# Graph attention and a normalised adjacency product: attention's transfers cut into tile-paced pieces, and the last z part of two sums put off

## What is computed

```python
# layer 0: attention with 16 heads of 32 columns
seq = (x @ W_seq).reshape(N, 16, 32)
score1, score2 = einsum(seq, a1), einsum(seq, a2)          # [head, row]
scores = leaky_relu(score1[:, :, None] + score2[:, None, :], 0.2)
scores = scores + (1.0 - adj)[None] * -65500.0
hidden = einsum('hij,jhd->ihd', softmax(scores, -1), seq).reshape(N, 512)
x = layernorm(x + elu(hidden @ W_out + b_out))
# layer 1: adj as coefficient and, symmetrised and normalised, as matrix
A = (adj + adj.T) * 0.5 + eye
A = dinv[:, None] * A * dinv[None, :]
x = layernorm(x + (adj @ A) @ x)
```

## Time and profile before

| | before |
|---|---|
| median of 3 runs | 788.06 us (787.59 to 788.43) |
| the profiled execution | 786.61 us |
| its span in the trace | 784.8 us |
| PE busy | 749.7 us (96%) |
| VectorE busy | 554.7 us (71%) |
| ScalarE busy | 409.9 us (52%) |
| GpSimd busy | 130.1 us (17%) |

### The profile page before, as it was taken

The page is one execution under the profiler, slowest core; times in us unless marked ns, Lnnn a source line. Parts: engine busy times, 40 slices in busy tenths (PEclk is TensorE's granted clock), DMA queues, the critical chain, the costliest instruction groups (busy, mean ns, idle before and its releaser), DMA issues.

```text
span 784.8 us, 29353 instructions
## 1 busy us (share of the span) xinstructions
PE 749.7 (96%) x13731; PEld 552.4 (70%) x13731; DVE 554.7 (71%) x799; ACT 409.9 (52%) x302; POOL 130.1 (17%) x142
## 2 busy tenths in 40 slices
PE   6999799988999999999999999999999999999997
PEld 2444699988999999999999999444434444444443
DVE  2887899998988999999999983687772211333233
ACT  2874887986977888788897880333321111000000
POOL 0000113012320211101111001364433100000000
PEclk9999799999999999999999999999999999999999
DMA  7992510255313111011110121599119800001111
GB/s 304 413 406 103 235 57 5 84 110 110 56 60 84 58 58 36 26 58 58 58 58 4 58 71 31 97 186 175 54 31 172 119 0 1 18 36 41 41 40 41
DMA packets 17770, 71.65 MB, mean 91 GB/s; under 512 B 2016, under 2 KB 2016, under 8 KB 13408
## 3 DMA queue, kind: packets, MB, share of 16 engines
q1 hardware_dynamic: 13040, 52.99, 17.7%
q0 software_dynamic: 4608, 16.78, 14.1%
HBM read 77.89 MB, written 8.65 MB: 110 GB/s over the span
## 4 chain that ended last, share of the span: by engine, by line
PE 78%; DVE 15%; issue 5%; ACT 1%; DMA 1%; POOL 0%; DVEq 0%; POOLq 0%; SPq 0%; ACTq 0%
PE bank L631 13%; PE bank L534 12%; PE bank L533 12%; PE bank L531 11%; PE bank L618 11%; PE bank L467 7%; PE bank L579 7%; DVE RZ L852 5%; PE bank L587 3%; DVE RG L871 2%; DVE RG L867 2%; DVE RP L816 1%; PE bank L571 1%; DVE MT L892 1%; DMA RZ<-in_L_gnn_W_seq_dram 1%
## 5 line engine op out<-in xcount | busy, mean ns | idle before, releaser
L531 PE MATMUL bank<-RP,RG 128*128 128x66 f16 x4096 | 388.8, 193 | 6.9 <-DVE RG L871 3.6
L534 PE MATMUL bank<-RP,MT 128*128 128x66 f16 x4096 | 388.7, 194 | 3.6 <-issue 3.6
L531 PEld LDWEIGHTS bank<-RP,RG 128*128 128x128 fp8e4 x4096 | 386.3, 98 | 8.3 <-DVE RG L871 3.6
L533 PE MATMUL bank<-RP,RG 128*128 128x66 f16 x4096 | 388.7, 195 | 2.1 <-issue 2.1
L534 PEld LDWEIGHTS bank<-RP,MT 128*128 128x128 fp8e4 x4096 | 386.4, 98 | 3.2 <-issue 3.2
L533 PEld LDWEIGHTS bank<-RP,RG 128*128 128x128 fp8e4 x4096 | 386.4, 97 | 2.7 <-issue 2.7
L689 ACT ACTIVATE RZ<-RZ,TAB 128x2048 int8<-128x2048 f32 x160 | 306.6, 1988 | 15.3 <-DVE RG L867 14.5
L852 DVE TENSOR_SCALAR RZ<-RZ,TAB 128x2048 int8<-128x2048 f32 x96 | 132.3, 1378 | 0.0
L867 DVE TENSOR_TENSOR RG<-RZ,MT 128x512 int32<-128x512 int32 x160 | 121.7, 760 | 0.1
L631 PE MATMUL bank<-RZ,MT 128*128 128x512 f16 x512 | 110.7, 379 | 2.2 <-DVE MT L1023 2.2
L391 POOL TENSOR_TENSOR RP<-SEQ,TAB 128x528 f32<-128x528 f32 x32 | 52.2, 1652 | 331.8 <-DVE RP L818 256.7
(11 more groups left out here) (103 smaller groups left out, 593.2 us busy)
## 6 DMA issues: line engine op xcount, KB each, us to landing
RG<-in_adj_t_dram SPq DMA_DIRECT2D x16, 1024.0 KB, 10.6
RZ<-s_rows_dram SPq DMA_DIRECT2D x16, 1024.0 KB, 5.8
seq_copy_dram<-SEQ SPq DMA_DIRECT2D x1, 4224.0 KB, 14.2
S2Q<-in_adj_p_dram POOLq DMA_DIRECT2D x8, 512.0 KB, 6.3
S2Q<-in_adj_tp_dram POOLq DMA_DIRECT2D x8, 512.0 KB, 11.3
RZ<-in_x_dram SPq DMA_DIRECT2D x16, 256.0 KB, 3.5
RP<-in_adj_p_dram POOLq DMA_DIRECT2D x8, 512.0 KB, 7.1
RP<-in_adj_tp_dram POOLq DMA_DIRECT2D x8, 512.0 KB, 13.8
```

The costliest lines, as they stand in the source:

```text
L531: mm(pb[bank][:, c:c + 2 * DV], step, high, start=(j == 0 and i % IB == 0), stop=(j == NT - 1), skip_group_check=True)
L533: mm(pb[bank][:, c:c + 2 * DV], step, low, start=False, stop=(j == NT - 1), skip_group_check=True)
L534: last = mm(pb[bank][:, c + DV:c + 3 * DV], mask, edge, start=False, stop=(j == NT - 1), skip_group_check=True)
```

## The change

The first four panels, the s1 rows, the copy of the sequence values and the output weights travel in pieces of a quarter (the copy: an eighth), and each piece but those of the first two rows waits for a value of `g_ready`, the count of masked tiles. Panel e is loaded in head 4 + 2e, accumulated in head 5 + 2e, and gets its diagonal after that; before, panel after panel followed in every head from `prep(3)` on. VectorE's wait for the copy moves from ahead of head 1 to the first `hidden_head`. In the last stage `take_back(t)` stands ahead of `low_z(t)`, the last of the 16 z parts of the first two output sums is added after both have their first 15, and panels 10 to 15 are loaded, accumulated and completed in a staggered order. `NE` = 4 replaces `NQ` in two places without a change of value.

```diff
+            def load_s1(h, q):
+                i = slice(q * (N // NS), (q + 1) * (N // NS))
+                sp.dma_start(S1B[:, h % 2, i], s1_rows[h:h + 1, i].broadcast_to([P, N // NS])).then_inc(s1b_in[h % 2], 16)
...
             sp.wait_ge(tabs_done, 1)
-            sp.dma_start(seq_copy[:, :], SEQ[:, :, :, :].rearrange("p t h d -> p (t h d)")).then_inc(seq_stored, 16)
-            with sp.Fori(1, H // 2) as p:
-                for u in range(2):
-                    h = p * 2 + u
-                    sp.wait_ge(z_ready, h * NV - NV)
-                    sp.wait_ge(g_ready, h * NT - NT)
-                    load_s1(h, u)
+            for q in range(NC):
+                sp.wait_ge(g_ready, q * (NT // NC))
+                ts = slice(q * (NT // NC), (q + 1) * (NT // NC))
+                sp.dma_start(seq_copy.rearrange("p (t h d) -> p t h d", t=NT, h=H)[:, ts, :, :], SEQ[:, ts, :, :]).then_inc(seq_stored, 16)
+            for h in range(2, H):
+                sp.wait_ge(z_ready, (h - 1) * NV)
+                for q in range(NS):
+                    sp.wait_ge(g_ready, (h - 1) * NT + 3 * q)
+                    load_s1(h, q)
...
-            sp.dma_start(WO, w_out.rearrange("(k p) d -> p k d", p=P)).then_inc(wout_in, 16)
+            for k in range(KC):
+                sp.wait_ge(g_ready, (H - 1) * NT + 3 * k)
+                sp.dma_start(WO[:, k, :], w_out[k * P:(k + 1) * P, :]).then_inc(wout_in, 16)
...
+            def load_pieces(t, h):
+                for q in range(NS):
+                    blocks = slice(q * (NT // NS), (q + 1) * (NT // NS))
+                    gp.wait_ge(g_ready, h * NT + 3 * q + 1)
+                    gp.dma_start(panel(t)[:, blocks, :], adj_p[t][:, blocks, :]).then_inc(panel_in[t], 16)
+
+            def add_pieces(t, h):
+                gp.wait_ge(panel_in[t], 16 * NS)
+                for q in range(NS):
+                    blocks = slice(q * (NT // NS), (q + 1) * (NT // NS))
+                    gp.wait_ge(g_ready, h * NT + 3 * q + 1)
+                    gp.dma_start(panel(t)[:, blocks, :], adj_tp[t][:, blocks, :], accum_op=ALU.add).then_inc(panel_sum[t], 16)
...
             for h in range(2, H):
                 prep(h)
-                if 3 <= h < 3 + NQ:
-                    load_panel(h - 3)
-                if 4 <= h < 4 + NQ:
-                    add_panel(h - 4)
-                if 5 <= h < 5 + NQ:
-                    add_diagonal(h - 5)
+                for e in range(NE):
+                    if h == 5 + 2 * e:
+                        load_pieces(e, h - 1)
+                    if h == 6 + 2 * e:
+                        add_pieces(e, h - 1)
+                    if h == 7 + 2 * e:
+                        add_diagonal(e, NS)
...
-            for t in range(NQ + NP, NT):
-                gp.wait_ge(y_ps, NQ if t < 2 * NQ + NP else t - NQ - NP + 1)
-                load_panel(t)
-            for t in range(NQ + NP, NT):
-                add_panel(t)
-            for t in range(NQ + NP, NT):
-                add_diagonal(t)
+            for t in range(NQ + NP, NT + 2):
+                if t < NT:
+                    gp.wait_ge(y_ps, t - NQ - NP + 1)
+                    load_panel(t)
+                if NQ + NP < t <= NT:
+                    add_panel(t - 1)
+                if NQ + NP + 1 < t:
+                    add_diagonal(t - 2)
...
-            for t in range(NT):
-                o_product(t)
+            for t in range(2):
+                o_product(t, range(NT - 1))
+            for t in range(2):
+                o_product(t, range(NT - 1, NT))
+            for t in range(2, NT):
+                o_product(t, range(NT))
...
             def hidden_head(h):
 
+                if h == 0:
+                    ve.wait_ge(seq_stored, 16 * NC)
...
-            ve.wait_ge(seq_stored, 16)
             att_head(1)
...
             for t in range(NT):
+                take_back(t)
                 low_z(t)
-                take_back(t)
```

More of the change, by code:

```diff
@@ L44, in gat_then_normalised_adjacency @@
     NQ = 4
+    NE = 4
+    NS = 4
+    NC = 8
     NP = 6
@@ L317, in _ @@
             sp.wait_ge(s1_stored, 16)
-            def load_s1(h, u):
-                sp.dma_start(S1B[:, u, :], s1_rows[DS(h, 1), :].broadcast_to([P, N])).then_inc(s1b_in[u], 16)
+            def load_s1(h, q):
+                i = slice(q * (N // NS), (q + 1) * (N // NS))
+                sp.dma_start(S1B[:, h % 2, i], s1_rows[h:h + 1, i].broadcast_to([P, N // NS])).then_inc(s1b_in[h % 2], 16)
             sp.wait_ge(seq_ps, NT)
-            load_s1(0, 0)
-            load_s1(1, 1)
+            for q in range(NS):
+                load_s1(0, q)
+            for q in range(NS):
+                load_s1(1, q)
             sp.wait_ge(tabs_done, 1)
-            sp.dma_start(seq_copy[:, :], SEQ[:, :, :, :].rearrange("p t h d -> p (t h d)")).then_inc(seq_stored, 16)
-            with sp.Fori(1, H // 2) as p:
-                for u in range(2):
-                    h = p * 2 + u
-                    sp.wait_ge(z_ready, h * NV - NV)
-                    sp.wait_ge(g_ready, h * NT - NT)
-                    load_s1(h, u)
+            for q in range(NC):
[7 more added lines that the diff above has]
+                    load_s1(h, q)
             sp.wait_ge(z_ready, (H - 1) * NV)
             sp.wait_ge(g_ready, (H - 1) * NT)
-            sp.dma_start(WO, w_out.rearrange("(k p) d -> p k d", p=P)).then_inc(wout_in, 16)
+            for k in range(KC):
+                sp.wait_ge(g_ready, (H - 1) * NT + 3 * k)
+                sp.dma_start(WO[:, k, :], w_out[k * P:(k + 1) * P, :]).then_inc(wout_in, 16)
             sp.dma_start(BB, b_out.rearrange("(o d) -> o d", o=1).broadcast_to([P, D])).then_inc(bb_in, 16)
@@ L406, in add_panel, with add_diagonal @@
                 gp.dma_start(panel(t), adj_tp[t], accum_op=ALU.add).then_inc(panel_sum[t], 16)
-            def add_diagonal(t):
-                gp.wait_ge(panel_sum[t], 16)
+            def load_pieces(t, h):
+                for q in range(NS):
+                    blocks = slice(q * (NT // NS), (q + 1) * (NT // NS))
[3 more added lines that the diff above has]
+                gp.wait_ge(panel_in[t], 16 * NS)
+                for q in range(NS):
+                    blocks = slice(q * (NT // NS), (q + 1) * (NT // NS))
+                    gp.wait_ge(g_ready, h * NT + 3 * q + 1)
+                    gp.dma_start(panel(t)[:, blocks, :], adj_tp[t][:, blocks, :], accum_op=ALU.add).then_inc(panel_sum[t], 16)
+            def add_diagonal(t, pieces=1):
+                gp.wait_ge(panel_sum[t], 16 * pieces)
                 diag = panel(t)[:, t, :]
@@ L561, in _ @@
                 general_products()
-            pe.wait_ge(wout_in, 16)
+            pe.wait_ge(wout_in, 16 * KC)
             pe.wait_ge(banks_free, H - 1)
@@ L584, in y_part @@
                 pe.wait_ge(xl_done, j + 1)
-                for i in range(NQ):
+                for i in range(NE):
                     for l in range(2):
@@ L605, in _ @@
                     pe.wait_ge(banks_free, H)
-                    pe.wait_ge(s2_done, NQ)
+                    pe.wait_ge(s2_done, NE)
                 if t >= LAG:
@@ L620, in y_product, with o_product @@
                 last.then_inc(y_ps, 1)
-            def o_product(t):
-                if t < 8:
+            def o_product(t, js):
+                if js[0] == 0 and t < 8:
                     pe.wait_ge(yv_done, t + 9)
-                else:
+                elif js[0] == 0:
                     pe.wait_ge(ov_done, t - 7)
-                for j in range(NT):
+                for j in js:
                     if t == 0:
@@ L632, in o_product @@
                                   start=(j == 0 and l == 0), stop=(j == NT - 1 and l == 1))
-                last.then_inc(o2_ps, 1)
+                if js[-1] == NT - 1:
+                    last.then_inc(o2_ps, 1)
             pe.wait_ge(v_added, NT)
-            for t in range(NQ, NT):
+            for t in range(NE, NT):
                 y_product(t)
             pe.wait_ge(mt_back, NT)
-            for t in range(NT):
-                o_product(t)
+            for t in range(2):
[4 more added lines that the diff above has]
+                o_product(t, range(NT))
         @block.scalar
@@ L682, in att_head @@
                 u = h % 2
-                sc.wait_ge(s1b_in[u], (h - u) * 8 + 16)
+                sc.wait_ge(s1b_in[u], (h // 2 + 1) * 16 * NS)
                 for j in range(NT):
@@ L848, in att_head @@
                 u = h % 2
-                ve.wait_ge(s1b_in[u], (h - u) * 8 + 16)
+                ve.wait_ge(s1b_in[u], (h // 2 + 1) * 16 * NS)
                 def own_step(m):
```

## The result

| | median | runs | span of the profiled run |
|---|---|---|---|
| before | 788.06 us | 787.08 to 788.43 (5) | 784.8 |
| after | 781.43 us | 779.23 to 783.98 (5) | 777.4 |

The ratio is 0.9919, with an interval from 0.9893 to 0.9945: some 6.6 us faster, where 13.6 were forecast, and 1.4 us above the top of the range. The five times spread over 4.8 us, before over 1.35. It is 6.2 us over that sum.

What follows compares the result with a forecast made beforehand. TensorE was taken as the bound, stalled by late code blocks behind transfers. Profiled run: 786.61 - 11.4 (stops) - 2.3 (end) + 0.1 (remaining loss) = 773.0 us; plus 1.45 to the median, forecast 774.5 us, range 772.5 to 780.

Steps and rivals of the forecast that it cites:

- the range: Whole kernel: median predicted between 772.5 and 780 us, meant to hold the forecast and rival A.
- that sum: Whole kernel: the predicted time of a profiled run, 786.61 - 11.4 - 2.3 + 0.1 = 773.0 us.
- The bound: Attention heads: TensorE stands still because its code blocks on queue 8 come late behind transfers; 11.4 us to gain.
- Rival B: Attention heads: code blocks were not the cause, so only the end's gain stays, 785.8 us; chance 0.06.
- How long a piece holds a block: Attention heads: hold proportional to size, 0.7 us per panel quarter, 1.0 per s1 quarter; 0.1 us of loss left.
- What TensorE bears: Attention heads: TensorE tolerates about 1.2 us of code block lateness and stops for the rest.
- rival A: Eight panel heads: panel and s1 pieces meet, stops remain, 4.6 us in all, giving 779 us; chance 0.13.
- One whole row per head costs nothing: Heads without a panel: code blocks come beside a whole s1 row of 144 packets, and nothing is lost.
- VectorE's lead: Tile 13, heads 2 and 3: VectorE's product ready 0.7 and 2.0 us before TensorE, so the whole 11.4 us fits.
- The pieces on their own queues: SyncE and GpSimd during attention: slower row landings and up to four extra issues per head cost zero.
- The end: Last stage: TensorE's idle time before its first output matmul goes, 2.3 us gained, panels 10 to 15 in time.
- Rival C: All heads: a piece holds a block by its landing, not its bytes; 16.8 us slower, 791 us; chance 0.05.

Runs made afterwards that it cites:

- tail_only: The kernel before with only the last stage changed: mask restored ahead of the low z part, two output sums in two parts; 784.52 us, ratio 0.9957.
- rows_whole: The changed kernel with whole s1 rows instead of quarters, panels still in quarters; 778.51 us, ratio 0.9872.
- panels_whole: The changed kernel with whole panel transfers in the same heads, s1 rows still in quarters; 789.27 us, ratio 1.0005.
- both_whole: The changed kernel with s1 rows and panels both whole, panels still in heads 4 to 11; 782.28 us, ratio 0.9950.
- row_later: early_drain with each whole s1 row released one VectorE comparison later; 776.71 us, ratio 0.9851.
- early_drain: rows_whole with a drain of GpSimd added ahead of its last loop, where it is idle; 776.87 us, ratio 0.9864.

## Why the prediction was right or wrong

**The bound** was right. The time lost in heads 2 to 5 was code blocks behind transfers, and it went when these were cut and moved. Rival B, that it was not the blocks, falls with tail_only: without the pieces all 12.3 us stay. That it is the code is read from the stops themselves, which lie where a block begins and are as long as its lateness less 1.6 us.

**How long a piece holds a block** is the step that failed. The prediction took it by proportion of bytes, 0.7 us for a panel quarter and 1.0 for a row quarter, and so left 0.1 us. Their bursts measured 1.9 and 2.0 us in the median, and one just ahead of a request held a block for about that long. A piece has the 144 packets of the whole, which is the likely reason. One row quarter alone is past the 1.4 us of lateness that TensorE bears, when it stands just ahead of a request; and instead of one chance per head there are four. What TensorE bears was judged well, 1.2 against 1.4. What was left is 4.1 us, which is rival A in place (heads 4 to 12, and the output weights in head 14) and nearly in size (4.6 us). In mechanism it is rival A in part: the pieces hold the blocks, but a meeting of both kinds is not needed, as the 1.65 us without panels show. It had a chance of 0.13. The rows could have warned: the earlier trace rows has 3.5 us for a quarter of the bytes that land in 5.8, which is three fifths and not a quarter. I took the bytes for what is in the way.

**One whole row per head costs nothing** was a second reading that went too far. It costs nothing where the block is asked for first, as in the earlier trace rows, and 1 us and more where it is not (rows_whole, head 9).

**VectorE's lead** was right to 0.1 us. The product of tile 13 of head 2:

```profile
158.70 1.57 DVE L899 TENSOR_TENSOR RG<-RZ,MT 128x512 int32<-128x512 int32 x1
...
161.00 0.19 PE L556 MATMUL bank<-RP,RG 128*128 128x66 f16 x1
```

It is ready at 160.27 and used at 161.00, 0.73 us later (predicted 0.7), and in head 3 2.06 us (predicted 2.0). VectorE was the limit nowhere after head 1.

**The pieces on their own queues.** SyncE's slower row and GpSimd's issues cost nothing during attention, as said: in a head with four accumulations VectorE was busy 22.96 us of 24.07, against 22.80 in the clean stretch, so four issues cost it 0.2 us at most. What was not looked at is GpSimd's last instruction. "Nothing behind it in the queue" was true for the work and false for the drain: 24 more transfers, 2.0 us more of drain, 1.8 of it past the cover of the last store. Without it the profiled run would be 777.4 us.

**The end.** 2.33 us gained against 2.3, and the panels were in time: TensorE waited for none of them between 575 and 670. "Nothing at the end moves" was right of the stores and wrong of the drain.

**Rival C**, that a piece holds a block by its landing, was nearer in that a hold is not by bytes, and had the wrong count: most blocks meet no burst at the wrong moment. It forecast 791 and stops in all heads; there were 4.1 us in nine.

**The range** ended at 780 because its upper end was rival A alone, 779. Rival A and the drain, 779 + 1.8, give 780.8, where the median is 781.4. The chances have a slip: the forecast, A and B add up to 0.95, not 0.94.

## What to carry to other kernels

Cutting a transfer along the free dimension left its number of packets as it was: here a quarter row took half of the queue time of a whole one and three fifths of its landing. As I read these runs, pieces help where the whole is far above what the waiting side bears, and they multiply the meetings. Panels in halves had 10.9 us of stops, in quarters 5.0, and the same quarters behind the row 3.5; smaller pieces were not tried. Count what an engine issued when looking at the end of a kernel: GpSimd's drain grew by 0.082 us per transfer, and a drain at an idle moment took its 1.8 us off the path.

## What the runs showed of the hardware

After each of the three stops of 2.7 us in panels_whole TensorE's granted clock was at its lower level (1.2 GHz) for 3.4 us. TensorE alone, behind the stop at 267.58 and in an undisturbed piece of the same length:

```profile
267.90:271.30 3.40, 3.40 (x73) 0.56 0.02 5
300.00:303.40 3.40, 3.37 (x109) 1.00 0.02 5
```

The 36 matmuls that are missing are another 1.1 us lost behind this stop. Behind the shorter stops of the other kernels, up to 2.3 us (both_whole), the clock stayed.

The runs of one kernel spread over as little as 0.9 us (row_later) and as much as 6.1 (both_whole); those of early_drain over 5.5. I put it on the order of burst and request, which turns over with a shift of tenths of a microsecond; only the profiled run of each kernel shows its stops, so this is argued and not shown.

The landing of a quarter row, 3.4 us, and of a whole, 5.8, make 0.8 us per 256 KB and 2.6 us that do not depend on the bytes. The Trainium skill, page "SBUF — State Buffer", section on the DMA setup-cost knee, has about 2 us for that part; the trace agrees in kind and is somewhat above.
